# Relative attention: two PSUM banks for the transposed weights, one for the dense jobs

## What is computed

```python
q = query @ Wq + bq;  k = key @ Wk + bk;  v = value @ Wv + bv      # key = value = context
attn1 = jnp.einsum('bhqd,bhkd->bhqk', rq, rk)
rel_k = rel_k_table[_rel_idx(t, s)]            # index: distance, clipped to +-32
attn2 = jnp.einsum('bhqd,qkd->bhqk', rq, rel_k)
attn = jax.nn.softmax((attn1 + attn2) / scale, axis=-1)
w1 = jnp.einsum('bhqk,bhkd->bhqd', attn, rv)
w2 = jnp.einsum('bhqk,qkd->bhqd', attn, rel_v)
x = (w1 + w2).transpose(0, 2, 1, 3).reshape(b, t, D_MODEL)
return x @ Wo + bo
```

## The kernel before

| group | jobs in order, with the engine that empties each |
|---|---|
| 0 | `xT` (ACT, L1926), `k0` (ACT, L1940), `q` (DVE, L2018), `k1` (ACT) |
| 1 | `r0` (ACT, L1932), `v0` (DVE, L2027), `r1` (ACT), none |
| 2 | `v1` (DVE), `den` (DVE, a reciprocal, L2030), `d0` (ACT, L1936), `d1` (ACT) |
| 3 | `w2` (DVE, L2033), `v2` (DVE), none, `out` (DVE, L2036) |

## Time and profile before

### The profile page before, as it was taken

How to read it: one execution, slowest core, us unless ns; L and a number is a source line. 1 busy time by engine, 2 the same in 40 slices (tenths; PEclk the granted TensorE clock), 3 DMA queues, 4 the chain that set the end, 5 groups by cost and what they waited for, 6 DMA issues and landing times. The chain is left out here.

```text
span 2960.7 us, 55727 instructions
## 1 busy us (share of the span) xinstructions
PE 2441.9 (82%) x19216; PEld 1937.4 (65%) x19216; DVE 1561.0 (53%) x2951; ACT 1236.9 (42%) x2780; POOL 614.9 (21%) x723
## 2 busy tenths in 40 slices
PE   5977999997899999938994899999999998497037
PEld 3656888886789999937773566666666666354025
DVE  3662555555711111137994466566566566544875
ACT  1121222222034333415663455555555555434744
POOL 1000111112634444415442111112111111000000
PEclk8997999997799999978996899999999999698569
DMA  3002222213479999940002655555555553121111
GB/s 91 22 6 74 58 50 52 58 50 114 160 256 346 343 345 343 345 144 12 0 0 41 141 120 117 123 116 117 124 115 118 125 114 91 41 83 50 70 69 39
DMA packets 386629, 346.64 MB, mean 117 GB/s; under 512 B 70508, under 2 KB 364934, under 8 KB 384518
## 3 DMA queue, kind: packets, MB, share of 16 engines
q1 hardware_dynamic: 374278, 329.03, 39.4%
q0 software_dynamic: 12288, 16.79, 2.6%
HBM read 258.72 MB, written 87.05 MB: 117 GB/s over the span
## 5 line engine op out<-in xcount | busy, mean ns | idle before, releaser
L1951 ACT COPY rel_probT<-rel_ps_t 121x400 f32<-121x400 f32 x384 | 196.3, 511 | 247.3 <-PE rel_ps_t L2168 247.3
L2168 PE MATMUL rel_ps_t<-rel_ident,rel_prob 100*121 100x100 f32 x1536 | 247.6, 284 | 34.7 <-ACT rel_probT L1951 34.7
L2168 PEld LDWEIGHTS rel_ps_t<-rel_ident,rel_prob 100*121 100x121 f32 x1536 | 196.1, 185 | 110.5 <-ACT rel_probT L1951 81.5
L1963 ACT ACTIVATE rel_prob<-rel_ps_s,rel_nmx 100x361 f32<-100x361 f32 x512 | 264.3, 579 | 2.8 <-DVE rel_nmx L2052 2.8
L1118 PEld LDWEIGHTS moe_ps_h<-moe_xeT,moe_w 128*128 128x128 f32 x2048 | 241.3, 194 | 5.1 <-issue 1.9
L1118 PE MATMUL moe_ps_h<-moe_xeT,moe_w 128*128 128x128 f32 x2048 | 241.9, 277 | 1.3 <-DVE moe_xeT L1283 1.3
L2052 DVE TENSOR_REDUCE rel_nmx<-rel_ps_s 100x2 f32<-100x722 f32 x256 | 232.8, 909 | 8.8
L1118 PE MATMUL moe_ps_y<-moe_w,moe_hT 128*128 128x256 f32 x1024 | 231.4, 379 | 0.0
L2681 PE MATMUL ffd_ps_y<-ffn_w_dT,ffd_oq 128*100 128x256 f32 x384 | 86.6, 387 | 145.7 <-DVE ffd_oq L2626 140.1
L1118 PEld LDWEIGHTS moe_ps_y<-moe_w,moe_hT 128*128 128x128 f32 x1024 | 189.6, 190 | 23.2
L1109 ACT ACTIVATE moe_hT<-moe_ps_h,moe_b 128x128 f32<-128x128 f32 x512 | 142.5, 375 | 141.8 <-PE moe_ps_h L1118 141.4
(11 more groups left out here) (427 smaller groups left out, 5230.2 us busy)
## 6 DMA issues: line engine op xcount, KB each, us to landing
moe_w<-in_L_ffn_w SPq DMA_DIRECT2D x128, 1024.0 KB
rel_scores<-rel_r_ext SPq DMA_DIRECT2D x32, 818.8 KB
rel_r_key<-rel_scores SPq DMA_DIRECT2D x32, 818.8 KB
rel_weights<-rel_prob SPq DMA_DIRECT2D x128, 204.7 KB
rel_by_dist<-rel_weights SPq DMA_DIRECT2D x32, 400.0 KB
mut_ctx_nat<-in_ctx SPq DMA_DIRECT2D x32, 363.0 KB
mut_ctx_T<-in_ctxT SPq DMA_DIRECT2D x32, 361.0 KB
rel_ctx_T<-in_ctxT SPq DMA_DIRECT2D x32, 361.0 KB, 4.2
```

The source lines that it names most:

```text
L1951: nc.scalar.copy(probT[:, pg % 2, c], ps_pT).then_inc(s_t_sb, 1)
L1963: last = nc.scalar.activation(prob[:, t.parity, slot, :], ps_s[0:S, j, 0:L], ACT.Exp, bias=nmx[:, slot:slot + 1])
L2168: last = nc.tensor.transpose(ps_pT[:, j, :], prob[:, pt.parity, QUAD * pg + j, c * STEP:c * STEP + R], ident[0:S, 0:S])
```

## The change

`ps_t` becomes two banks and the transposes alternate between them: transposes n wait for the copy of n-2 in place of n-1. `ps_m` becomes one bank: each dense job waits until the job right before it has been emptied. The two semaphores `bank0_emptied` and `bank1_emptied` become one, `bank_emptied`, with its counts over all jobs. Every engine of the stage keeps its matmuls, copies, vector and DMA instructions in the same order, with the same sizes; what differs is what they wait for (and some register instructions). The other stages are the same.

```diff
-        ps_m = m.ps("ps_m", [P, 2, 512])
+        ps_m = m.ps("ps_m", [P, 512])
         ps_s = m.ps("ps_s", [P, QUAD, 512])
-        ps_t = m.ps("ps_t", [P, 512])
+        ps_t = m.ps("ps_t", [P, 2, 512])
         ps_o = m.ps("ps_o", [P, 512])
-        ps_pT = ps_t[0:R, 0:QUAD * S].rearrange("p (j s) -> p j s", j=QUAD)
+        ps_pT = [ps_t[0:R, v, 0:QUAD * S].rearrange("p (j s) -> p j s", j=QUAD) for v in range(2)]
...
-        s_job, s_job_sb = sem("banks_filled"), [sem(f"bank{v}_emptied") for v in range(2)]
+        s_job, s_job_sb = sem("bank_filled"), sem("bank_emptied")
...
-            eng.wait_ge(s_job_sb[n % 2], before(t, n, n % 2) + 1)
+            eng.wait_ge(s_job_sb, before(t, n) + 1)
...
-                nc.scalar.copy(probT[:, pg % 2, c], ps_pT).then_inc(s_t_sb, 1)
+                nc.scalar.copy(probT[:, pg % 2, c], ps_pT[(CH * pg + c) % 2]).then_inc(s_t_sb, 1)
...
-                o = before(t, n, n % 2)
+                o = before(t, n)
                 if not isinstance(o, int) or o > 0:
-                    pe.wait_ge(s_job_sb[n % 2], o)
-                out = bank(what)
+                    pe.wait_ge(s_job_sb, o)
+                out = ps_m
...
-                if not isinstance(n, int) or n > 0:
-                    pe.wait_ge(s_t_sb, n)
+                if not isinstance(n, int) or n > 1:
+                    pe.wait_ge(s_t_sb, n - 1)
                 for j in range(QUAD):
-                    last = nc.tensor.transpose(ps_pT[:, j, :],
+                    last = nc.tensor.transpose(ps_pT[(CH * pg + c) % 2][:, j, :],
```

More of the change, by code:

```diff
@@ L1748, in relative_cross, with share, before @@
         NUMBER = {what: n for n, (_, what) in enumerate(JOBS)}
[L1750 to L1761, removed]
+        ps_two = ps_m[:, 0:KC * S].rearrange("p (c s) -> p c s", c=KC)
+        def share(n, kind):
+            return sum(who == kind for who, _ in JOBS[:n])
+        def before(t, n):
             nj = len(JOBS)
             if isinstance(t.i, int):
-                return sum(share(nj, v, kind) * min(max(t.i + ahead, 0), B) + ((t + ahead).within(B) and share(n, v, kind))
+                return sum(share(nj, kind) * min(max(t.i + ahead, 0), B) + ((t + ahead).within(B) and share(n, kind))
                            for kind, ahead in AHEAD.items())
-            return (t.i * sum(share(nj, v, kind) for kind in AHEAD)
-                    + sum(share(nj, v, kind) * ahead + share(n, v, kind) for kind, ahead in AHEAD.items()))
+            return (t.i * sum(share(nj, kind) for kind in AHEAD)
+                    + sum(share(nj, kind) * ahead + share(n, kind) for kind, ahead in AHEAD.items()))
         def wait_filled(eng, t, what):
@@ L1925, in empty @@
                 if what == "xT":
-                    nc.scalar.copy(xT[:], two(what)).then_inc(s_job_sb[n % 2], 1)
+                    nc.scalar.copy(xT[:], ps_two).then_inc(s_job_sb, 1)
                 elif what in ("r0", "r1"):
@@ L1932, in empty @@
                     nc.scalar.copy(r_ext[:, h * HC:(h + 1) * HC, LEFT:NEAR],
-                                   bank(what)[0:S, 0:HC * ND].rearrange("p (h r) -> p h r", h=HC)).then_inc(s_job_sb[n % 2], 1)
+                                   ps_m[0:S, 0:HC * ND].rearrange("p (h r) -> p h r", h=HC)).then_inc(s_job_sb, 1)
                 elif what in ("d0", "d1"):
                     h = int(what[1])
-                    nc.scalar.copy(distT[:, h * PAIRS // 2:(h + 1) * PAIRS // 2, :], bank(what)[:, 0:PAIRS // 2 * S].rearrange(
-                        "p (n s) -> p n s", n=PAIRS // 2)).then_inc(s_job_sb[n % 2], 1)
+                    nc.scalar.copy(distT[:, h * PAIRS // 2:(h + 1) * PAIRS // 2, :], ps_m[:, 0:PAIRS // 2 * S].rearrange(
+                        "p (n s) -> p n s", n=PAIRS // 2)).then_inc(s_job_sb, 1)
                 else:
                     c = int(what[1])
-                    nc.scalar.activation(kT[:, b.parity, c, :], bank(what)[:, 0:L], ACT.Identity,
-                                         bias=k_bias[:, c:c + 1]).then_inc(s_job_sb[n % 2], 1)
+                    nc.scalar.activation(kT[:, b.parity, c, :], ps_m[:, 0:L], ACT.Identity,
+                                         bias=k_bias[:, c:c + 1]).then_inc(s_job_sb, 1)
             def transposed(pt, pg, c):
@@ L2017, in empty @@
                         dve.wait_ge(s_qh, b.i - 1)
-                    nc.vector.scalar_tensor_tensor(out=qT[:, b.parity], in0=two(what), scalar=SCALE,
+                    nc.vector.scalar_tensor_tensor(out=qT[:, b.parity], in0=ps_two, scalar=SCALE,
                                                    in1=bq_scaled[:].unsqueeze(2).to_broadcast([P, KC, S]),
-                                                   op0=ALU.mult, op1=ALU.add).then_inc(s_job_sb[n % 2], 1)
+                                                   op0=ALU.mult, op1=ALU.add).then_inc(s_job_sb, 1)
                 elif what in ("v0", "v1", "v2"):
@@ L2026, in empty @@
                     halves = vals[:, b.parity, c].rearrange("p (k e) (x d) -> p k (e x) d", e=2, x=2)[:, :, 0:4:3, :]
-                    nc.vector.tensor_tensor(halves, bank(what)[0:R, 0:D].rearrange("p (k e d) -> p k e d", k=PAIRS, e=2),
-                                            v_bias[:].rearrange("p (k e) d -> p k e d", e=2), ALU.add).then_inc(s_job_sb[n % 2], 1)
+                    nc.vector.tensor_tensor(halves, ps_m[0:R, 0:D].rearrange("p (k e d) -> p k e d", k=PAIRS, e=2),
+                                            v_bias[:].rearrange("p (k e) d -> p k e d", e=2), ALU.add).then_inc(s_job_sb, 1)
                 elif what == "den":
-                    nc.vector.reciprocal(rec[:], two(what)).then_inc(s_job_sb[n % 2], 1)
+                    nc.vector.reciprocal(rec[:], ps_two).then_inc(s_job_sb, 1)
                 elif what == "w2":
                     wait_emptied(dve, t, "den")
-                    nc.vector.tensor_tensor(attT[:], two(what), rec[:], ALU.mult).then_inc(s_job_sb[n % 2], 1)
+                    nc.vector.tensor_tensor(attT[:], ps_two, rec[:], ALU.mult).then_inc(s_job_sb, 1)
                 elif what == "out":
                     dve.wait_ge(s_xb, b.i + 1)
-                    nc.vector.tensor_tensor(at(y_nat, b.i), bank(what)[0:S, 0:D], at(y_nat, b.i), ALU.add).then_inc(s_job_sb[n % 2], 1)
+                    nc.vector.tensor_tensor(at(y_nat, b.i), ps_m[0:S, 0:D], at(y_nat, b.i), ALU.add).then_inc(s_job_sb, 1)
                     wait_emptied(dve, t, what)
@@ L2099, in fill @@
                     for c in range(KC):
-                        last = nc.tensor.transpose(two(what)[:, c, :], xn[:, c * P:(c + 1) * P], ident[0:S, 0:S])
+                        last = nc.tensor.transpose(ps_two[:, c, :], xn[:, c * P:(c + 1) * P], ident[0:S, 0:S])
                 elif what == "q":
@@ L2104, in fill @@
                         for k in range(KC):
-                            last = mm(two(what)[:, c, :], w["Wq"][:, k, c * P:(c + 1) * P], xT[:, k, :], k, KC)
+                            last = mm(ps_two[:, c, :], w["Wq"][:, k, c * P:(c + 1) * P], xT[:, k, :], k, KC)
                 elif what in ("r0", "r1"):
@@ L2129, in fill @@
                     for e in range(2):
-                        last = mm(two(what), swap[:, e, :], raw[:].rearrange("p (c e) s -> p e c s", e=2)[:, e], e, 2)
+                        last = mm(ps_two, swap[:, e, :], raw[:].rearrange("p (c e) s -> p e c s", e=2)[:, e], e, 2)
                 elif what == "w2":
                     for e in range(2):
-                        nc.tensor.matmul(two(what), pick[:, e, :], raw[:].rearrange("p (c e) s -> p e c s", e=2)[:, e],
+                        nc.tensor.matmul(ps_two, pick[:, e, :], raw[:].rearrange("p (c e) s -> p e c s", e=2)[:, e],
                                          start=(e == 0), stop=False)
@@ L2136, in fill @@
                     for q in range(QUAD):
-                        last = nc.tensor.matmul(two(what), tab_v_wide[:, q, :],
+                        last = nc.tensor.matmul(ps_two, tab_v_wide[:, q, :],
                                                 distT[:].rearrange("p (c q) s -> p q c s", c=KC)[:, q],
```

## The result

The changed kernel takes 3124.89 us (median of 4, 3123.76 to 3137.34) against 2959.70: ratio 1.0568 with a 95% interval of 1.0541 to 1.0595, 165 us slower. The forecast was 3110 within 3035 to 3140. The profiled execution is the slowest of the four, 3137.34 us with a span of 3135.6, so its rows show some 12 us more than the median.

The account below looks back on a forecast made before the run. The prediction took TensorE to bound relative attention (busy 732.96 of 800 us). Waits of 84 us gave 3044 us on the median, and 66 us for a falling clock made 3110, range 3035 to 3140.

Parts of the forecast that it names:

- 84 us of waits: New waits less the saved one in relative attention: 2.68 us a turn times 29, plus 6 us for the opening turns.
- Group 2: Third of a turn's four parts: den waits for v1, d0 for the reciprocal, d1 for ACT's copy; 2.36 us lost a turn.
- Group 0 and 1: First two parts of a turn: q and k1 wait, 0.89 us; r1 waits for v0's emptying, 0.16 us left.
- Group 3: Last part of a turn: the third transposes no longer wait for the copy, so xT starts earlier; 0.73 us gained a turn.
- Opening and closing turns: Dense jobs packed closely in the opening turns cost some 6 us more; gain and loss taken as equal in turns 0 and 30 to 32.
- The clock: TensorE's clock falls to half in most turns, slow over d1, the scores and w2: 2.2 us times 30, 66 us.
- That the clock holds: Rival: TensorE's clock does not fall, so only the waits cost time; 3044 us, chance 0.24.
- That half of the stalls go into slack: Rival: in group 2 den loses nothing or group 3 catches up, 2.36 becomes about 1.3 us; 3013 us, chance 0.06.
- That it is faster: Rival: every wait for the transposes' copies is on the path and dense jobs are emptied behind transposes; about 2930 us, chance 0.03.

Follow-up runs that it names:

- e2: e1 plus spare matmuls into the unused eighth bank, one before den's wait, two before d0's, two before xT's: 3059.74 us, ratio 1.0356.
- e7: The changed kernel, but DVE empties v1 between the two maxima of group 2 in place of after both: 3064.79 us, ratio 1.0353.
- e6: The changed kernel, but DVE first copies den out of the bank and takes the reciprocal from the copy: 3072.04 us, ratio 1.0396.
- e8: The changed kernel with the edits of e3, e6 and e7 together: 2989.49 us, ratio 1.0117 to the kernel before.
- e3: The changed kernel, but GpSimd's far waits until DVE has written xn: 3065.23 us, ratio 1.0374.
- e4: The kernel before the change, but GpSimd's far waits until DVE has written xn: 2950.08 us, ratio 0.9984.
- e5: The changed kernel with the transposes back at one bank and far waiting for xn: 3096.99 us, ratio 1.0466.
- e1: The changed kernel with the transposes back at one bank, the dense jobs still sharing one: 3071.11 us, ratio 1.0403.

## Why the prediction was right

- **Sign and size.** The two terms were 84 us of waits and 66 of clock. Measured with e2 the waits are 105, and the clock 62 to 65. So the clock's term was right and that of the waits 20 us short, which the range took in. A turn costs 2.98 us more at full clock (forecast 2.68), and 2.22 more by the clock (forecast 2.2). Within the 2.68 two errors of opposite sign stood: a gain of 0.73 that was not there, and 0.4 us too much in groups 1 and 2.
- **Group 2**, forecast 2.36 us: by the starts of the scores of groups 2 and 3 it is 8.04 us (2030.51 to 2038.55) for 5.99, so 2.05. The places were right: `v1` behind the maxima, the reciprocal, then ACT. e7, e6 and e8 show each. What was over is the hand-over time: the reciprocal and `distT` began 0.04 us after the end of their matmuls, not 0.13 (which holds for `q`), and `distT` took 0.49 us, not 0.53.
- **Group 0 and 1**, forecast 0.89 and 0.16: 0.88 (from `xT` to the scores of group 1 6.76 us for 5.88) and 0.06. These are read from the traces; no run takes the waits of group 0 away.
- **Group 3**, forecast a gain of 0.73: nothing by `xT`. The next scores do come 0.36 us sooner (7.40 for 7.76), and `xT` then waits that much longer. This is the step that failed. It read "`out`, DVE's sum, `xn` and `xT` all move up with it". `out` and the sum did; `xn` could not end before `far`, and `far` hangs on the exponentials. e3 and e4 show it, and e5 shows the bank's real worth, 0.9 us, once that is out of the way.
- **Opening and closing turns**, forecast 6 us: 105 less 28 turns of 2.98 leaves some 20. Against the trace of the kernel before, that of e2 is 4 us longer between the stage's first `xT` and the 28 turns, 8 behind them, and 4 ahead of that first `xT`; what these consist of stays open. This is the other term that was too small.
- **The clock.** Size right, place only in part, so the match of the size is partly luck. The forecast put all slow time over the end of group 2 and `w2`. 18 of the 27 stretches are there; 9 begin at `xT`, where idle time grew (0.47 and 1.48 us) and the forecast had it shrink. And e1 shows what the forecast would have denied: at the same length of a full-clock turn, one bank less is some 50 us faster.
- **Rivals.** That the clock holds (3044) is excluded by the result, and e2 shows that 3060 is what it would have been. That half of the stalls go into slack (3013) is excluded by e2. That it is faster is excluded by the result.

## What to carry to other kernels

A single bank costs little only when its emptying is quick and early. Write down for each job who empties it and what stands ahead on that engine's list: here `v1` stood behind the maxima (0.79 us), and in e6 `distT` behind the exponentials (0.84 us), both beyond the copy's own length. Ask of each saved wait who else holds the next step; here an engine off the path, GpSimd, held it. And idle time has a place: 0.48 and 1.48 us close together at the turn of the loop went with 9 falls of TensorE's clock, 0.63 and 1.12 us further apart with none. So look at the clock before trusting a sum of waits.

## What the runs showed that I had not expected

- DVE's `xn`, a `tensor_scalar` of 100 x 256, takes 0.40 us alone, 0.79 and 1.70 us when `far` is running on GpSimd, in the steady turns to 0.15 us after its end. A wait that starts GpSimd's work later made two kernels faster.
- 5 spare matmuls a turn made a kernel 11 us faster (e1 to e2), by keeping the clock at 2.4 GHz; from e1 to e5 less waiting made one some 20 us slower.
- A slow stretch of 6.8 us costs 2.9 us (turns of 33.5 for 30.6), one of 3.4 us 1.6 (32.2 for 30.6 in e1).
